# A GRU of 256 steps on one core, without the warm-up matmul that TensorE runs in each step

## The chip, the core and the metric

The kernel runs on one NeuronCore of a Trainium2 chip. The core has four engines that compute: TensorE (PE) for matmuls, VectorE (DVE), ScalarE (ACT) and GpSimd (POOL), and a fifth one, SyncE (SP), which issues transfers. Each engine works off its own list of instructions in order and waits for the others through semaphores. TensorE's clock is granted at one of two levels, 2.4 or 1.2 GHz; the profile writes them as 1.00 and 0.50. The metric is the device time of one execution in microseconds (us).

## The reference, cut to what matters

Two transformer-like layers run over x (4 batches, 256 positions, 256 features) and a vector cond (4 x 256): attention with normalised heads, attention with quantised heads, a resampling with a sparse feed-forward net, then a GRU over the 256 positions, causal attention on its outputs, a small block attention with a layer norm, and a routed feed-forward net. The change touches the GRU alone:

```
def cell(h, x):                      # x: (4, 256) of one position, h: (4, 256)
    gi = x @ W_ih + b_ih             # 256 x 768
    gh = h @ W_hh + b_hh             # 256 x 768
    i_r, i_z, i_n = split(gi, 3);  h_r, h_z, h_n = split(gh, 3)
    r = sigmoid(i_r + h_r);  z = sigmoid(i_z + h_z)
    n = tanh(i_n + r * h_n)
    return (1 - z) * n + z * h
```

The first h is cond. Every position needs the h of the one before, so the 256 steps can't overlap.

## The kernel before

The program has six phases; a barrier between two of them (`next_round`) makes each engine wait for the other three. The GRU is the fourth and has no loop on the chip: its 256 steps are written out, in eight tiles of 32 positions. Its four engines each have a function: `gru_pe`, `gru_act`, `gru_dve`, `gru_pool`.

The four batch rows are too few to fill TensorE's 128 columns. So a gate's 256 outputs are cut into pieces that go to four column groups of 32. `gate` (L827) issues, for each of the two halves of h and each of four column groups, one f32 matmul with 4 columns of weights (the state) and 64 moving columns (a part of W_hh). The trace shows each of these as two records, so the three gates of a step are 48 records, all on L831.

One step t runs like this:

- PE waits for the state (`g_h`) and issues the r gate into one bank, the n gate into the second, the z gate into the third. Each adds to what ScalarE has put there before: the input's share (for n, the bias).
- VectorE transposes the r gate's sums (L969), then the n gate's (L973). ScalarE takes the sigmoid of r (L898).
- VectorE runs a scan that forms i_n + r * h_n in `pre_n` (L978). ScalarE takes the tanh (L906) into `nzh`.
- Meanwhile ScalarE takes the sigmoid of the z gate (L902), and VectorE transposes it (L980).
- ScalarE puts the next step's input shares into the banks (L871, three copies); the first of them stands between L902 and L906 in its order.
- VectorE's last scan (L987) writes the new state into `h_ring` and raises `g_h`; a small product (L942) prepares the next step's `nzh`.

After the z gate PE does one more thing in each step. In seven of the eight tiles, at positions 2 and 4 it does half of the next tile's input matmuls for r and z (`rows_in`, L814, four f32 matmuls with 512 moving columns, eight records), and at positions 6 and 8 those for n (`cols_in`, L821, two f32 matmuls with 128 moving columns, four records). In every other step it runs a warm-up matmul: `keep_warm(1, pM[2])` (L860) issues one bf16 matmul of zeros, 128 x 128 by 512 columns, into a bank that nobody reads in this phase. Its record carries the helper's line, L286. The other phases call `keep_warm` too, with 3, 6 or 8 matmuls at their own places.

Nothing waits for the warm-up matmul, and it waits for nothing; PE works it off in its order, between the z gate of one step and the wait for the next state.

Of the kernel before, what the change touches and what calls it, by code (L numbers as in the profile page):

```python
# [64 lines left out]
def build(nc, d, out):  # L65

    ctx = ExitStack()
    with ctx:
# [84 lines left out]
        pS, pT, pO, pM = bank[0:2], bank[2:4], bank[4], bank[5:8]  # L153
# [119 lines left out]
        def next_round(eng, n):  # L273

            for s in (rd_pe, rd_act, rd_dve, rd_pool):
                eng.wait_ge(s, n)

        def end_round(eng, last, n, rd):

            eng.wait_ge(last, n)  # L280
            eng.sem_inc(rd, 1)

        def keep_warm(n, bank):

            for _ in range(n):
                nc.tensor.matmul(bank[:, :], zero16[:, 0:P], zero16[:, :], start=True, stop=True, skip_group_check=True)  # L286
# [363 lines left out]
        def phase3_pe(pe):  # L650
# [11 lines left out]
            with pe.Fori(0, B) as i:  # L662
# [36 lines left out]
                down(1)  # L699
                end_round(pe, s_down, i * 2 + 2, rd_pe)  # L700
            gru_pe(pe)

        def phase3_act(act):
# [94 lines left out]
        def h_col(t, c):  # L798

            return h_ring[:, h_at(t):h_at(t) + 24].rearrange("p (b x) -> p b x", b=B)[:, :, 3 * c + 2]  # L800
# [9 lines left out]
        def gru_pe(pe):  # L810
            def rows_in(tile, k):
                for b in range(B):
                    at = b * S + tile * TILE
                    mm = nc.tensor.matmul(bank_g[32 * b:32 * b + 32, :], xT[:, k, at:at + TILE], w_ih[:, k, 0:2 * D],  # L814
                                          start=(k == 0), stop=(k == KC - 1), skip_group_check=True)
                if k == KC - 1:
                    mm.then_inc(g_gi, 1)

            def cols_in(tile, m):
                for k in range(KC):  # L820
                    mm = nc.tensor.matmul(bank_i[:, m * P:(m + 1) * P], w_ih[:, k, 2 * D + m * P:2 * D + (m + 1) * P],  # L821
                                          xT[:, k, :].rearrange("p (b s) -> p b s", b=B)[:, :, tile * TILE:(tile + 1) * TILE],
                                          start=(k == 0), stop=(k == KC - 1), skip_group_check=True)
                if m == KC - 1:
                    mm.then_inc(g_ni, 1)

            def gate(t, bank, g, seed, done):  # L827
                pe.wait_ge(seed, t + 1)
                for c in range(KC):
                    for j in range(4):  # L830
                        mm = nc.tensor.matmul(bank[32 * j:32 * j + B, 0:64], h_col(t, c),  # L831
                                              w_hh[:, c, g, :].rearrange("p (m n) -> p m n", m=KC)[:, :, 32 * j:32 * j + 32],
                                              start=False, stop=(c == KC - 1), skip_group_check=True)
                mm.then_inc(done, 1)

            next_round(pe, 13)
            for bank in (bank_r, bank_n, bank_z):
                mm = nc.tensor.matmul(bank[:, 0:64], zero16[:, 0:P], zero16[:, 0:64], start=True, stop=True, skip_group_check=True)
            mm.then_inc(g_open, 1)
            pe.wait_ge(ld_hh, 16)  # L840
            for k in range(KC):
                rows_in(0, k)
            for m in range(KC):
                cols_in(0, m)
            for t in range(S):
                tile, u = divmod(t, TILE)
                pe.wait_ge(g_h, t + 1)
                gate(t, bank_r, 0, g_sdr, g_rm)
                gate(t, bank_n, 2, g_sdn, g_nm)
                gate(t, bank_z, 1, g_sdz, g_zm)  # L850
                if tile + 1 < TILES and u in (2, 4):
                    if u == 2 and tile:
                        pe.wait_ge(g_gd, 4 * tile + 4)
                    rows_in(tile + 1, u // 2 - 1)
                elif tile + 1 < TILES and u in (6, 8):
                    if u == 6:
                        pe.wait_ge(g_nd, tile + 1)
                    cols_in(tile + 1, u // 2 - 3)
                else:
                    keep_warm(1, pM[2])  # L860
            end_round(pe, g_zm, S, rd_pe)
            phase5_pe(pe)

# [131 lines left out]
        def phase5_pe(pe):  # L995
            def project(n, t):

                if t == 0:
                    pe.wait_ge(s_stage3, n)
                for o, w0, w1 in ((pM[t][:, :], 0, 2 * D), (pM[2][:, t * D:(t + 1) * D], 2 * D, 3 * D)):  # L1000
                    for k in range(KC):
                        mm = nc.tensor.matmul(o, aT[:, k, t * P:(t + 1) * P], w_qkv3[:, k, w0:w1],  # L1002
                                              start=(k == 0), stop=(k == KC - 1), skip_group_check=True)
                mm.then_inc(s_qkv3, 1)

            next_round(pe, 14)
            pe.wait_ge(ld_w3, 16)
            for t in range(ST):
                project(1, t)
            with pe.Fori(0, B) as i:  # L1010
                keep_warm(6, pT[0])
                pe.wait_ge(rd_act, i + 14)
                pe.wait_ge(rd_dve, i + 14)
                head_rows(pe, i + 8, extra=6)
                pe.wait_ge(s_vcp, i + 5)
                attn_pe(pe, 8, i, causal=True, ahead=lambda t: project(i + 2, t))
                out_proj(pe, i, 8, w_out3)
                end_round(pe, s_proj, i + 9, rd_pe)
            phase6_pe(pe)
# [564 lines left out]
```

## Time and profile before

| | |
|---|---|
| median of 3 runs | 1282.61 us (1279.76 to 1285.07) |
| the profiled execution | 1276.65 us |
| its span, from the first to the last instruction | 1274.8 us |
| mean granted clock of TensorE | 0.949 |
| PE busy with matmuls | 941.4 us (74%) |
| DVE, ACT, POOL busy | 849.8 us (67%), 521.5 us (41%), 50.9 us (4%) |
| L831, the gates: busy, PE's idle time before them | 221.4 us, 182.7 us |
| L286, all warm-up matmuls: records, busy | 528, 166.8 us |

A line such as "L831 PE MATMUL banks<-w_qkv,h_ring 128*4 128x64 f32 x12288 | 221.4, 221 | 182.7 <-DVE h_ring L987 157.7" is read so: the line of the code, the engine, the operation, what it writes and reads by the program's names (the recurrent weights live in the buffer of `w_qkv2`, hence the name), the shapes, the number of records; then busy time in us and the mean of one in ns; then the idle time of the engine just before them and who ended most of it. The line PEclk shows the granted clock in 40 equal slices of the span, in tenths. In the chain that ended last the profile goes back from the last instruction to what released it, and so on, and gives each line its share of the span.

### The profile page before, as it was taken

The numbers are of one execution on the slowest core, as the hardware profiler recorded it, in microseconds if no ns is written. First come the engines' busy times: TensorE is split into PE (matmuls) and PEld (weight loads), VectorE is DVE, ScalarE is ACT, GpSimd is POOL, SyncE is SP. The second block draws the span as 40 slices with busy tenths as digits, with TensorE's granted clock in tenths as the row PEclk, the third lists the DMA queues.
The fourth block names the chain that finished last, engine by engine and source line by source line (L and its number), as shares of the span: only waits on it lengthen the run. The fifth ranks groups of instructions, "written<-read, shape, count | busy, mean of one in ns | idle before, by whom it ended". The sixth has DMA issues, their size and how long they took to land.

```text
span 1274.8 us, 41104 instructions
## 1 busy us (share of the span) xinstructions
PE 941.4 (74%) x16529; PEld 619.4 (49%) x16529; DVE 849.8 (67%) x2611; ACT 521.5 (41%) x2096; POOL 50.9 (4%) x115
## 2 busy tenths in 40 slices
PE   2899899867877888736666666666666669999836
PEld 2567566434443555514444444444444447776525
DVE  5767576576774666747677776767676657767664
ACT  2435354324441111125555555555555534544211
POOL 0000000022220000100000000000000000000000
PEclk9899999969998999969999999999999999999958
DMA  7000000010001000000000000000000000000101
GB/s 256 3 1 0 0 0 0 0 67 0 0 0 67 0 0 0 33 9 13 4 12 4 13 4 12 4 12 7 10 9 7 4 3 1 0 0 0 34 0 33
DMA packets 32230, 19.77 MB, mean 16 GB/s; under 512 B 23120, under 2 KB 29264, under 8 KB 32080
## 3 DMA queue, kind: packets, MB, share of 16 engines
q1 hardware_dynamic: 32080, 17.64, 4.9%
q8 instruction: 110, 1.80, 0.6%
q14 instruction: 40, 0.33, 0.1%
HBM read 14.49 MB, written 1.05 MB: 12 GB/s over the span
## 4 chain that ended last, share of the span: by engine, by line
PE 38%; DVE 29%; issue 21%; ACT 6%; POOL 2%; DMA 1%; SPq 1%; DVEq 1%; POOLq 0%; ACTq 0%
PE banks L831 9%; PE banks L313 6%; DVE work L973 5%; DVE gate_r L969 5%; DVE h_ring L987 4%; ACT nzh L906 4%; DVE pre_n L978 4%; PE banks L348 3%; PE banks L674 2%; PE banks L1002 2%; PE banks L360 2%; PE banks L1381 2%; PE banks L687 1%; PE banks L286 1%; DVE work L772 1%
## 5 line engine op out<-in xcount | busy, mean ns | idle before, releaser
L831 PE MATMUL banks<-w_qkv,h_ring 128*4 128x64 f32 x12288 | 221.4, 221 | 182.7 <-DVE h_ring L987 157.7
L831 PEld LDWEIGHTS banks<-w_qkv,h_ring 128*4 128x4 f32 x12288 | 173.9, 88 | 266.0 <-DVE h_ring L987 242.8
L286 PE MATMUL banks<-zero 128*128 128x512 bf16 x528 | 166.8, 391 | 10.2 <-DVEq L1554 4.2
L313 PE MATMUL banks<-shared,qT 128*128 128x256 f32 (+2 forms) x640 | 154.3, 349 | 9.4 <-DVE nraw L441 3.6
L898 ACT ACTIVATE zr<-gate_r 128x8 f32<-128x8 f32 x256 | 55.7, 217 | 205.2 <-DVE gate_r L969 205.2
L417 ACT ACTIVATE probs_b<-banks,nraw 128x256 f32<-128x256 f32 (+1 forms) x256 | 100.0, 445 | 76.1 <-DVE nraw L441 43.3
L969 DVE STREAM_TRANSPOSE gate_r<-banks 128x64 f32<-128x64 f32 x256 | 63.9, 250 | 90.8 <-PE banks L831 87.5
L313 PEld LDWEIGHTS banks<-shared,qT 128*128 128x128 f32 (+1 forms) x640 | 95.3, 174 | 30.6 <-DVE nraw L441 12.7
L441 DVE TENSOR_REDUCE nraw<-banks 128x2 f32<-128x512 f32 x128 | 84.9, 686 | 12.0 <-PE banks L313 11.4
L286 PEld LDWEIGHTS banks<-zero 128*128 128x128 bf16 x528 | 50.6, 98 | 68.4 <-issue 21.2
L451 DVE COPY work<-banks 128x512 f32<-128x512 f32 (+1 forms) x104 | 64.1, 616 | 19.9 <-PE banks L360 16.9
L973 DVE STREAM_TRANSPOSE work<-banks 128x64 f32<-128x64 f32 x256 | 76.3, 298 | 0.7 <-PE banks L831 0.7
L348 PE MATMUL banks<-cst,probs_b 128*128 128x128 f32 x448 | 72.2, 278 | 5.0 <-ACT probs_b L417 2.9
L987 DVE TENSOR_TENSOR_SCAN h_ring<-zz,nzh 128x24 f32<-128x24 f32 x256 | 53.2, 208 | 26.6 <-ACT nzh L906 0.5
L980 DVE STREAM_TRANSPOSE zz<-gate_z 128x64 f32<-128x64 f32 x256 | 69.1, 270 | 1.1 <-issue 0.6
L978 DVE TENSOR_TENSOR_SCAN pre_n<-zr,work 128x16 f32<-128x16 f32 x256 | 49.0, 191 | 27.0 <-DVE work L973 0.9
L348 PEld LDWEIGHTS banks<-cst,probs_b 128*128 128x128 f32 x448 | 50.2, 141 | 26.1 <-issue 10.9
L906 ACT ACTIVATE nzh<-pre_n 128x8 f32<-128x8 f32 x256 | 54.8, 214 | 16.7 <-DVE pre_n L978 1.0
L871 ACT COPY banks<-big 128x64 f32<-128x64 f32 x256 | 53.8, 210 | 12.5 <-DMA big<-big 12.5
L902 ACT ACTIVATE gate_z<-banks 128x64 f32<-128x64 f32 x256 | 57.4, 224 | 1.7 <-PE banks L831 1.4
L871 ACT COPY banks<-bhn 128x64 f32<-128x64 f32 x256 | 54.0, 211 | 0.0
L871 ACT COPY banks<-work 128x64 f32<-128x64 f32 x256 | 53.8, 210 | 0.0
(282 smaller groups left out, 1421.2 us busy)
## 6 DMA issues: line engine op xcount, KB each, us to landing
big<-in_x SPq DMA_DIRECT2D x1, 1024.0 KB, 5.6
w_gate<-in_L_ffn_w_gate SPq DMA_DIRECT2D x1, 1024.0 KB, 10.2
shared<-in_L_ffn_w_up SPq DMA_DIRECT2D x1, 1024.0 KB, 5.4
shared<-in_L_ffn_w_down SPq DMA_DIRECT2D x1, 1024.0 KB, 7.9
w_gate<-in_L_ffn_W SPq DMA_DIRECT2D x1, 1024.0 KB, 6.2
big<-big SPq DMA_DIRECT2D x64, 16.0 KB
work<-big SPq DMA_DIRECT2D x64, 16.0 KB
shared<-in_L_ffn_W SPq DMA_DIRECT2D x1, 1024.0 KB, 7.0
```

What stands on the lines that cost most here:

```text
L286: nc.tensor.matmul(bank[:, :], zero16[:, 0:P], zero16[:, :], start=True, stop=True, skip_group_check=True)
L313: mm = nc.tensor.matmul(out, qT[:, c, tile], k[:, c, 0:n], start=True, stop=not causal, skip_group_check=True)
L348: mm = nc.tensor.transpose(pSK[h % 2][:, o:o + P], by_q[h % 3][:, qt * S + kt * P:qt * S + (kt + 1) * P], ident)
L417: a = nc.scalar.activation(by_q[h % 3][:, o:o + n], pSQ[h % 3][:, o:o + n], ACT.Exp, bias=nraw[:, t, h:h + 1])
L441: m = nc.vector.tensor_reduce(nraw[:, :, h], pSQ[h % 3].rearrange("p (t k) -> p t k", t=ST), AX.X, ALU.max, negate=True)
L831: mm = nc.tensor.matmul(bank[32 * j:32 * j + B, 0:64], h_col(t, c), w_hh[:, c, g, :].rearrange("p (m n) -> p m n", m=KC)[:, :, 32 * j:32 * ...
L871: return nc.scalar.copy(bank[:, 0:64], rows).then_inc(done, 1)
L906: nc.scalar.activation(every(nzh[:, :], 0, 3), every(pre_n[:, :], 1), ACT.Tanh, scale=-1.0).then_inc(g_th, 1)
L969: nc.vector.transpose(gate_r[:, :], bank_r[:, 0:64]).then_inc(g_tr, 1)
L973: nc.vector.transpose(blocks(npair[:, 16 * (t % RING):16 * (t % RING) + 128], 0), bank_n[:, 0:64].rearrange("p (m n) -> p m n", m=KC)).the ...
L978: nc.vector.tensor_tensor_scan(pre_n[:, :], zr[:, :], npair[:, 16 * (t % RING):16 * (t % RING) + 16], 0.0, ALU.mult, ALU.add).then_inc(g_p ...
L987: nc.vector.tensor_tensor_scan(h_ring[:, h_at(t + 1):h_at(t + 1) + 24], zz[:, 0:24], nzh[:, :], 0.0, ALU.mult, ALU.subtract).then_inc(g_h, 1)
```

## The change

The `else` branch in the loop of `gru_pe` goes, and with it the call of `keep_warm(1, pM[2])`. In steps without input matmuls PE has nothing between the z gate and the next wait. The other engines' code, the input matmuls and the `keep_warm` calls of the other phases stay.

```diff
--- before.py
+++ after.py
@@ -856,8 +856,6 @@
                     if u == 6:
                         pe.wait_ge(g_nd, tile + 1)
                     cols_in(tile + 1, u // 2 - 3)
-                else:
-                    keep_warm(1, pM[2])
             end_round(pe, g_zm, S, rd_pe)
             phase5_pe(pe)
```

## Rows read from the trace of the kernel before

**Rows 1.** The page: span, granted clock in 40 slices, chain that ended last.
```profile
span 1274.8 us, 41104 instructions
...
PEclk9899999969998999969999999999999999999958
...
PE banks L831 9%; PE banks L313 6%; DVE work L973 5%; DVE gate_r L969 5%; DVE h_ring L987 4%; ACT nzh L906 4%; DVE pre_n L978 4%; PE banks L348 3%; PE banks L674 2%; PE banks L1002 2%; PE banks L360 2%; PE banks L1381 2%; PE banks L687 1%; PE banks L286 1%; DVE work L772 1%
```

**Rows 2.** Groups of instructions, 560 to 1040 us: busy us, mean ns, idle before.
```profile
L831 PE MATMUL banks<-w_qkv,h_ring 128*4 128x64 f32 x12288 | 221.4, 221 | 182.7 <-DVE h_ring L987 157.7 <-ACT banks L871 23.0
...
L286 PE MATMUL banks<-zero 128*128 128x512 bf16 x228 | 89.3, 392 | 0.0
```

**Rows 3.** Line L831 alone: duration min/median/max, first and last start.
```profile
L831 PE MATMUL banks<-w_qkv,h_ring x12288: 219/219/314, 562.0 to 1037.5; 128*4 128x64 f32 x199
```

**Rows 4.** Order of time, one step at the high clock: start us, duration us.
```profile
648.61 0.86 PE L831 MATMUL banks<-w_qkv,h_ring 128*4 128x64 f32 x48 [0.67 <-DVE h_ring L987]
...
649.31 0.30 DVE L973 STREAM_TRANSPOSE work<-banks 128x64 f32<-128x64 f32 x1
...
649.39 0.39 PE L286 MATMUL banks<-zero 128*128 128x512 bf16 x1
...
649.71 0.19 DVE L978 TENSOR_TENSOR_SCAN pre_n<-zr,work 128x16 f32<-128x16 f32 x1
...
650.19 0.21 DVE L987 TENSOR_TENSOR_SCAN h_ring<-zz,nzh 128x24 f32<-128x24 f32 x1
...
650.45 0.86 PE L831 MATMUL banks<-w_qkv,h_ring 128*4 128x64 f32 x48 [0.66 <-DVE h_ring L987]
```

**Rows 5.** Order of time, the loop's second step, at the low clock.
```profile
564.46 1.47 PE L831 MATMUL banks<-w_qkv,h_ring 128*4 128x64 f32 x48 [0.42 <-DVE h_ring L987]
...
565.57 0.30 DVE L973 STREAM_TRANSPOSE work<-banks 128x64 f32<-128x64 f32 x1 [0.18 <-PE banks L831]
...
565.86 0.44 PE L286 MATMUL banks<-zero 128*128 128x512 bf16 x1
565.97 0.19 DVE L978 TENSOR_TENSOR_SCAN pre_n<-zr,work 128x16 f32<-128x16 f32 x1
565.99 0.23 ACT L902 ACTIVATE gate_z<-banks 128x64 f32<-128x64 f32 x1 [0.35 <-PE banks L831]
566.12 0.22 ACT L871 COPY banks<-big 128x64 f32<-128x64 f32 x1
...
566.26 0.21 ACT L906 ACTIVATE nzh<-pre_n 128x8 f32<-128x8 f32 x1
...
566.65 0.21 DVE L987 TENSOR_TENSOR_SCAN h_ring<-zz,nzh 128x24 f32<-128x24 f32 x1
...
566.91 0.85 PE L831 MATMUL banks<-w_qkv,h_ring 128*4 128x64 f32 x48 [0.61 <-DVE h_ring L987]
```

**Rows 6.** Order of time on PE, input matmuls of two steps.
```profile
567.58 1.04 PE L814 MATMUL banks<-w_ih,xT 128*32 128x512 f32 x8
...
578.78 0.71 PE L821 MATMUL banks<-xT,w_ih 128*128 128x128 f32 x4
```

**Rows 7.** Order of time on PE, a step that began later than its neighbours.
```profile
789.31 0.86 PE L831 MATMUL banks<-w_qkv,h_ring 128*4 128x64 f32 x48 [0.97 <-DVE h_ring L987]
```

**Rows 8.** Stretches: busy us (records) of PE, PEld, DVE, ACT, POOL; clock; DMA.
```profile
788.00:791.00 3.00, 1.52 (x53) 0.81 (x50) 2.03 (x10) 1.76 (x12) 0.00 (x0) 1.00 0.04 8
791.50:794.50 3.00, 2.58 (x81) 1.86 (x75) 1.66 (x7) 0.96 (x7) 0.00 (x0) 0.50 0.00 0
337.00:340.00 3.00, 1.63 (x13) 1.01 (x14) 2.73 (x6) 0.10 (x1) 1.21 (x6) 1.00 0.00 0
341.00:344.00 3.00, 2.98 (x16) 1.75 (x15) 2.17 (x5) 1.84 (x4) 0.44 (x3) 0.50 0.00 0
276.00:282.00 6.00, 5.64 (x27) 3.12 (x28) 4.68 (x10) 2.75 (x4) 1.17 (x6) 0.50 0.00 0
562.00:565.50 3.50, 3.04 (x91) 2.35 (x95) 1.66 (x7) 1.20 (x9) 0.00 (x0) 0.50 0.00 0
```

## The prediction

> **What bounds the kernel now.** I read the page first [rows 1]. The span is 1274.8 us, the line of granted clocks stands at 9 from one end to the other apart from single slices, and the chain that ended last goes through L831, the gates' matmuls, at 9%, then through the VectorE and ScalarE lines of the same loop, none of them above 5%. So the GRU is a chain over several engines; no engine is full in it. The groups of instructions between 560 and 1040 us [rows 2] give the counts: 12288 matmul records on L831 are 48 for each of the 256 steps, and 228 warm-up matmuls stand there, one for each step but 28. PE sits idle 182.7 us before L831, and before L286 it never idles. L831 runs from 562.0 to 1037.5 us [rows 3]: 475.5 us for 255 step distances, 1.865 us each, 37% of the span.
>
> Then I read the order of time for one step at the high clock [rows 4] and for one at the low clock [rows 5], because the first two steps of the loop happen to have run at the low one. In rows 4 the reader is to see the ring: L831 starts at 648.61, L973 can read the n gate at 649.31 (0.70 later), L978 runs at 649.71, L987 writes the new state at 650.19, and L831 starts again at 650.45. That is 1.84 us. The warm-up matmul starts at 649.39 and takes 0.39, so it is over at 649.78, and PE then waits 0.66 us for the state. It is on no path: it is PE's last work of the step and the next thing in PE's queue is a wait for L987.
>
> **The change part by part.** It takes 228 matmuls of 0.392 us, 89.3 us of PE's busy time, out of 228 steps [rows 2].
>
> Direct cost of what goes: nothing of it was on the path, so nothing comes back. The cover is 0.66 us of idle time behind each one at the high clock; at the low clock [rows 5] the one at 565.86 is over at 566.30 and PE still waits 0.61 us. Bounds: below, a gain. A few steps of the loop are longer than 1.84 us (L831 at 789.31 came after 0.97 us of idle time, not 0.66 [rows 7]). If every such excess were the warm-up's doing, it would be all of 255 x (1.865 - 1.84) = 6 us, of which some 2 belong to four steps at the low clock; so a gain of 4 us at most. I see no wait of theirs on PE and take 0.
>
> Indirect cost: what PE's clock does. Without the warm-up, PE works 0.86 us in each 1.84, 47%, where it now works 0.86 + 0.39, 68%. What did the engine do before the clock fell elsewhere? In the same loop, from 788 to 791 us, a single longer step brought PE to 1.52 us of 3.00, 51%, with the warm-up still in it, and at 791 the clock went to 0.50 [rows 8]. In another stage PE was busy 1.63 of 3.00 us, 54%, from 337 to 340 us, and from 341 on the clock was at 0.50 [rows 8]. So 47%, step after step, is under two levels at which it fell. I take it that it falls, and soon, in every row of plain steps.
>
> Does it come back? Between 276 and 282 us the clock was at 0.50 with PE busy 5.64 of 6.00 us, 94% [rows 8]; the loop's start shows 3.04 of 3.50 us, 87%, at 0.50, and 791.5 to 794.5 shows 2.58 of 3.00, 86%; the clock rose right behind both. A step at the low clock without the warm-up has 1.47 us of PE in 2.45 (from 564.46 to 566.91 [rows 5]), 60%. That is less than any stretch here after which it rose, so plain steps keep the low clock. The 28 steps with input matmuls are another thing: L814 has eight matmuls, 1.04 us, and L821 four, 0.71 us, at the high clock [rows 6]. At the low one L814 is some 2.1 us, and with the gates' 1.47 PE is full for a whole step. They sit at positions 2, 4, 6 and 8 of each tile of 32, for seven tiles. I expect the clock to rise at the first or second of them, and to stay up a step or two after the last: from position 3 to 10 or 11, 8 or 9 of 32 steps.
>
> A step at the low clock costs 2.45 us (564.46 to 566.91) against 1.84: +0.61. The rows say where. L973 starts 1.11 us behind L831 instead of 0.70, +0.41, since the r and n gates take longer. And L987 starts 0.68 behind L978 instead of 0.48, +0.20, because L902 waits for the z gate to 565.99, then L871 has ScalarE, and L906 starts only at 566.26. Around 791 to 796 the distances were a little shorter, since the clock changed inside them, so I use 0.60.
>
> Sum: 256 steps less 7 x 8.5 = 60 at the high clock leaves 196; four of those are at the low clock already; 192 x 0.60 = 115 us. In one heavy step of each tile L814 runs at the low clock: from about 1.3 us behind the start, 2.1 us long, 3.4 instead of 2.45, +1.0; the clock changes inside some, so seven of these give some 4 us. Together +119. The profiled execution of before took 1276.65 us, 1.85 around its span; plus 119 is 1396. The median of its runs, 1282.61, lies 6 above it. I forecast a median of 1400 us.
>
> A rule of the Trainium skill speaks against this. "TensorE: Matmul & The Clock Gate", section "Why this matters for your kernels", says that throughput drops in the middle of a kernel are avoided by leaving no idle gap of about 3 us between bursts of matmuls. The longest gap in a step here would be about 1 us, so by that rule the warm-up is needless and the time stays at 1283. The trace does not agree: before the fall at 791 us no gap of PE was longer than 0.97 us. I give the rule the chance of the rival below.
>
> **The rivals.**
> The clock stays high. For it: from 562 to 1038 us it did so but for the loop's start and one fall, although PE was idle about a third of the time, and the loop has steps with much more work in each tile. Against it: the fall at 51%. Its place is PE, its price is the 0 to -4 us of above, and it decides if 0.86 us of work in 1.84 are enough. Time 1279 to 1283.
> The clock swings all the time: it falls in plain steps and comes back in plain steps too. For it: at the low clock PE's share rises from 47% to 60% by itself, and that is more than the 54% of the other fall. Against it: the low clock of 276 to 282 us with PE at 94%. If every second step is slow, 126 x 0.60 = 76 us: 1359.
> The clock never comes back after its first fall. Then 252 x 0.61 = 154, plus 14 steps with L814 at +1.0 and 14 with L821 at +0.3 (1.3 + 1.4 = 2.7 against 2.45), 18 us: +172, 1455. Against it: heavy steps fill PE for a whole step, and after full stretches it rose each time.
>
> **How the numbers follow.** Forecast 0.72, swinging 0.12, never back 0.08, stays high 0.08 (0.06 of it no change, 0.02 a gain over 0.5%, for which 6 us would be needed). I take 0.5% as what a measurement of this kernel tells from no change, since its three runs lie within 0.4%. In the forecast itself one step more or less per tile at the high clock is 4 us and a slow step of 0.55 or 0.65 is 10 us; 6 or 12 fast steps per tile make it 1411 or 1385. The range takes in the swinging case: 1345 to 1430. Faster 0.02, same 0.06, slower 0.92.
>
> **What would show it.** In the changed kernel the slices of the GRU should show a clock of 5 to 7 tenths in each, not 9, and a bit higher at each tile's beginning. The groups should have 300 L286 records instead of 528, the mean of L831 well above 221 ns, and the stretch of L831 should be near 595 us, not 475.5. In the order of time plain steps should be 2.4 to 2.45 us apart with L973 1.1 us behind L831. All stages but the GRU should keep their lengths. I am wrong if the GRU's slices stay at 9, and wrong on the size if plain steps without an input matmul run at the high clock far behind position 11 of a tile, or if not even positions 3 to 10 do.

## The result, and the profile after

The kernel without the warm-up matmul took 1394.17 us in the median of six runs (1388.04 to 1401.27), the kernel before beside it 1283.23 us (1279.76 to 1288.15). The ratio is 1.0868, with a 95% interval of 1.0834 to 1.0902: 111 us more. The forecast was 1400 us, with a range of 1345 to 1430. All ratios in this document leave out executions more than 1.5% above the fastest one of the same kernel.

The page of the changed kernel, the same three things as [rows 1]:

```profile
span 1386.2 us, 40620 instructions
...
PEclk9899999799989997757667656556575558999957
...
PE banks L831 22%; PE banks L313 6%; DVE h_ring L985 4%; DVE zz L978 4%; PE banks L348 3%; ACT gate_z L900 3%; PE banks L674 2%; PE banks L1000 2%; PE banks L360 2%; PE banks L1379 2%; DVE work L971 1%; DVE gate_r L967 1%; ACT nzh L904 1%; PE banks L687 1%; DVE pre_n L976 1%
```

The granted clock is 5 to 7 in every slice of the GRU, where it was 9; outside the GRU it is as it was but for single slices (the slice at the GRU's start was low before, too). In the chain, L831 has gone from 9% to 22%. (Lines behind the change stand two numbers lower: L987 is L985 now.)

The line L831 alone, and its group of instructions from the page (busy us, mean ns, idle before), which answer to [rows 3] and [rows 2]:

```profile
L831 PE MATMUL banks<-w_qkv,h_ring x12288: 219/311/314, 562.8 to 1147.2; 128*4 128x64 f32 x199
```
```profile
L831 PE MATMUL banks<-w_qkv,h_ring 128*4 128x64 f32 x12288 | 330.0, 283 | 255.0 <-DVE h_ring L985 229.0
```

From its first to its last record L831 took 1147.2 - 562.8 = 584.4 us, where it took 475.5: 108.9 of the 111.4 us by which the span grew. The median of one record is 311 ns, not 219. The matmuls are the same 12288; they ran mostly at 1.2 GHz (the mean granted clock from 562 to 1149 us is 0.62). Of the 2.5 us left, 0.9 us stands in the first matmuls of the next phase (the 16 of L1000 took 7.85 us, 6.95 before).

How many steps were slow can be read from the waits. At the high clock ScalarE does not wait for the z gate, at the low clock it does; columns are total us, times, longest. Before:

```profile
ACT gate_z L902 <- PE banks L831: 1.4, 4, 0.4
```

After:

```profile
ACT gate_z L900 <- PE banks L831: 64.5, 185, 0.4
DVE work L971 <- PE banks L831: 31.8, 180, 0.2
```

So 180 to 185 steps met the low clock, fully or in part, where 4 did before.

The order of time in one slow step, which answers to [rows 5]:

```profile
700.92 1.47 PE L831 MATMUL banks<-w_qkv,h_ring 128*4 128x64 f32 x48 [0.98 <-DVE h_ring L985]
...
702.02 0.30 DVE L971 STREAM_TRANSPOSE work<-banks 128x64 f32<-128x64 f32 x1 [0.18 <-PE banks L831]
...
702.42 0.19 DVE L976 TENSOR_TENSOR_SCAN pre_n<-zr,work 128x16 f32<-128x16 f32 x1
702.45 0.22 ACT L900 ACTIVATE gate_z<-banks 128x64 f32<-128x64 f32 x1 [0.35 <-PE banks L831]
702.57 0.22 ACT L869 COPY banks<-work 128x64 f32<-128x64 f32 x1
702.70 0.29 DVE L978 STREAM_TRANSPOSE zz<-gate_z 128x64 f32<-128x64 f32 x1
702.71 0.21 ACT L904 ACTIVATE nzh<-pre_n 128x8 f32<-128x8 f32 x1
...
703.10 0.21 DVE L985 TENSOR_TENSOR_SCAN h_ring<-zz,nzh 128x24 f32<-128x24 f32 x1
...
703.36 1.47 PE L831 MATMUL banks<-w_qkv,h_ring 128*4 128x64 f32 x48 [0.98 <-DVE h_ring L985]
```

It is 2.44 us long against 1.84. PE waits 0.98 us of it for the state; its own work, 1.47 us, is the longer part of the ring. The chain that ended last, in the same step:

```profile
700.92 1.51 PE banks L831 x48
702.43 0.02 issue
702.45 0.23 ACT gate_z L900
702.68 0.02 issue
702.70 0.30 DVE zz L978
...
703.10 0.22 DVE h_ring L985
```

Here all 48 records stand in it. In a fast step only the r gate's 16 do, as the chain of the kernel before has it:

```profile
650.45 0.45 PE banks L831 x16
```

The stretches around one tile (the second) show when the clock rose and fell. A heavy step is one with input matmuls, a plain step one without. The first stretch holds the end of the tile before and the tile's start; columns are as in [rows 8]:

```profile
636.00:641.00 5.00, 3.47 (x100) 2.62 (x104) 2.94 (x13) 2.00 (x14) 0.00 (x0) 0.50 0.02 5
645.00:656.00 11.00, 7.21 (x313) 5.14 (x304) 8.02 (x39) 5.79 (x36) 0.00 (x0) 1.00 0.01 3
656.00:664.00 8.00, 3.70 (x219) 2.85 (x204) 5.79 (x28) 4.29 (x26) 0.00 (x0) 1.00 0.02 5
664.00:667.00 3.00, 1.03 (x63) 0.77 (x60) 2.20 (x11) 2.33 (x13) 0.00 (x0) 1.00 0.15 22
670.00:708.00 38.00, 22.47 (x740) 17.89 (x730) 22.00 (x94) 14.98 (x96) 0.93 (x2) 0.50 0.04 6
```

The clock comes up at the input matmuls. PE is then 66% busy until they are done (7.21 of 11.00 us), and in the plain steps behind them 46% and less (3.70 of 8.00 us, then 1.03 of 3.00). The clock stays high for some of these steps and then falls. At the low clock PE is 59% busy (22.47 of 38.00) and stays there for the rest of the tile.

### The profile page after: what moved, and what is told of

Same layout as the page of the kernel before. It is cut to its first block, busy times and chain, and to the rows that moved or that the text cites. A ratio compares the mean times of both kernels' runs of the same rounds, so it can differ in the third digit from the quotient of the medians.

```text
span 1386.2 us, 40620 instructions
## 1 busy us (share of the span) xinstructions
PE 978.4 (71%) x16273; PEld 690.6 (50%) x16301; DVE 873.4 (63%) x2611; ACT 516.6 (37%) x2096; POOL 50.8 (4%) x115
## 4 chain that ended last, share of the span: by engine, by line
PE 49%; DVE 21%; issue 19%; ACT 6%; POOL 2%; DMA 1%; SPq 1%; DVEq 0%; POOLq 0%; ACTq 0%
PE banks L831 22%; PE banks L313 6%; DVE h_ring L985 4%; DVE zz L978 4%; PE banks L348 3%; ACT gate_z L900 3%; PE banks L674 2%; PE banks L1000 2%; PE banks L360 2%; PE banks L1379 2%; DVE work L971 1%; DVE gate_r L967 1%; ACT nzh L904 1%; PE banks L687 1%; DVE pre_n L976 1%
## 5 line engine op out<-in xcount | busy, mean ns | idle before, releaser
L831 PE MATMUL banks<-w_qkv,h_ring 128*4 128x64 f32 x12288 | 330.0, 283 | 255.0 <-DVE h_ring L985 229.0
L831 PEld LDWEIGHTS banks<-w_qkv,h_ring 128*4 128x4 f32 x12288 | 264.7, 112 | 333.3 <-DVE h_ring L985 306.0
L978 DVE STREAM_TRANSPOSE zz<-gate_z 128x64 f32<-128x64 f32 x256 | 73.2, 286 | 16.9 <-ACT gate_z L900 0.6
L900 ACT ACTIVATE gate_z<-banks 128x64 f32<-128x64 f32 x256 | 57.1, 223 | 64.7 <-PE banks L831 64.5
L286 PE MATMUL banks<-zero 128*128 128x512 bf16 x272 | 71.1, 390 | 13.2 <-PE banks L533 4.5
L985 DVE TENSOR_TENSOR_SCAN h_ring<-zz,nzh 128x24 f32<-128x24 f32 x256 | 53.1, 208 | 26.5 <-ACT nzh L904 0.5
L869 ACT COPY banks<-big 128x64 f32<-128x64 f32 x256 | 54.6, 213 | 14.4 <-DMA big<-big 14.4
L869 ACT COPY banks<-bhn 128x64 f32<-128x64 f32 x256 | 55.5, 217 | 0.0
L869 ACT COPY banks<-work 128x64 f32<-128x64 f32 x256 | 54.7, 214 | 0.0
L940 DVE TENSOR_TENSOR nzh<-h_ring,signs 128x16 f32<-128x16 f32 x256 | 44.8, 175 | 10.2 <-ACT zr L884 1.0
```

Source lines behind the costliest of these rows:

```text
L869: return nc.scalar.copy(bank[:, 0:64], rows).then_inc(done, 1)
L900: nc.scalar.activation(gate_z[:, :], bank_z[:, 0:64], ACT.Sigmoid, scale=-1.0).then_inc(g_sz, 1)
L978: nc.vector.transpose(blocks(zz[:, :], 2, 3), gate_z[:, :].rearrange("p (m n) -> p m n", m=KC)).then_inc(g_tz, 1)
L985: nc.vector.tensor_tensor_scan(h_ring[:, h_at(t + 1):h_at(t + 1) + 24], zz[:, 0:24], nzh[:, :], 0.0, ALU.mult, ALU.subtract).then_inc(g_h, 1)
```

## The experiments

Theory W says that the clock follows how much PE streams (how many columns its matmuls move through the array), and that the level of the clock is the whole of the loss. Against it stood: P, that any PE instruction in the idle gap would do; S, that the longest gap decides; G, that each step without a warm-up pays for itself; D, that the loss is not the clock's at all. All ratios are to the kernel before, run beside each.

**A warm-up of 32 columns (e1_cols32).**

```diff
-                    keep_warm(1, pM[2])
+                    nc.tensor.matmul(pM[2][:, 0:32], zero16[:, 0:P], zero16[:, 0:32], start=True, stop=True, skip_group_check=True)
```

> The warm-up matmul stands at its old place in all 228 steps, but with 32 moving columns instead of 512; its weights are loaded as before. Theory W (the clock follows how much of the time PE streams): the idle gap before the next state is broken at the same place, but PE works hardly more than in the changed kernel, so the GRU runs mostly at the low clock and the time is that of the changed kernel, 1385 to 1400 us, with some 180 steps of 2.44 us. Rival P (any PE instruction at that place, or the weight load with it, keeps the clock): about 1283 us, the GRU's slices at 9 tenths. Rival D (what was lost is not the clock but something the instruction did for its neighbours): the steps return to 1.84 us, whatever the clock shows.

Measured: 1393.63 us, ratio 1.0888 (1.0832 to 1.0944). The groups of instructions of this kernel from 560 to 1150 us:

```profile
L831 PE MATMUL banks<-w_qkv,h_ring 128*4 128x64 f32 x12288 | 327.2, 281 | 222.1 <-DVE h_ring L987 198.1 <-ACT banks L871 23.2
...
L860 PE MATMUL banks<-zero 128*128 128x32 bf16 x228 | 46.3, 203 | 0.0
```

All 228 warm-ups are there, each counted as 203 ns busy, and they bring nothing. That rules out P: neither an instruction in the gap nor its weight load keeps the clock. D falls as well: the instruction is back at its place, and yet the records of L831 are at the low clock (281 ns in the mean) and the time stays lost. It also warns of the busy column, which gives the 32 columns 203 ns and the 512 columns 392 [rows 2], though they stream sixteen times as many.

**256 columns (e2_cols256)**, the same edit with 256.

> The warm-up with 256 moving columns instead of 512 in all 228 steps. At the high clock that is some 0.11 us of streaming less of the 0.21 that the full one streams. Theory W in a strict form (the change of clock is a switch and not a slope): half the work does not bring half of the gain. PE's work per plain step is then nearer to that of the changed kernel than to that of the kernel before, the one fall of the kernel before came with a step only 0.3 us too long, and I expect it to fall in nearly every tile and to come back at the input matmuls only: 1375 to 1395 us. Theory W as a slope: half of the 111 us, about 1338 us. Rival P: 1283 us.

Measured: 1289.08 us, ratio 1.0063 (1.0035 to 1.0091). My range of 1375 to 1395 us missed it by 86 us. The strict form had the switch on the wrong side of 256 columns; the slope was wrong too. Half of the warm-up does 93% of its work (8 us lost of 111). The kernel is less even, though: its ten executions lie between 1279.9 and 1309.0 us, and the longest has the lowest mean granted clock, 0.907 against 0.945. The wait of L902 for the z gate came 21 times in this kernel's GRU:

```profile
ACT gate_z L902 <- PE banks L831: 7.2, 21, 0.4
```

**128 and 192 columns (e7_cols128, e9_cols192)**, the same edit, to find the edge.

> The warm-up with 128 moving columns in all 228 steps, between the 256 that kept the clock for nearly all of the loop and the 32 that did nothing. Theory W as a switch: PE then streams 0.05 us more per plain step than in the changed kernel. I expect the clock to fall in each tile as there, perhaps a few steps later, and to come back at the input matmuls or, in some tiles, before: 1350 to 1392 us, nearer to the upper end. If the loss were a slope in the columns, 256 columns at +8 us and 32 at +113 would put 128 at about +68 us, 1348 us.

Measured: 1378.26 us, ratio 1.0747 (1.0701 to 1.0793); 163 such waits. As forecast for a switch (1350 to 1392), and well above the slope (1348).

> The warm-up with 192 moving columns, between the 128 that cost 97 us and the 256 that cost 8. If the loss goes in a switch, one of the two neighbours is repeated or the loop swings between them tile by tile; I expect falls in nearly every tile, but returns inside a tile too, since with 128 columns a few of those were there already: 1300 to 1350 us. On a straight line between the neighbours it would be 1334 us, so this run places the switch and does not prove its form.

Measured: 1365.53 us, ratio 1.0665 (1.0581 to 1.0748), from two executions, and a miss: it is 16 us above my range of 1300 to 1350. It shows the form all the same: by the ratios 0, 32, 128, 192, 256 and 512 columns cost 111, 114, 96, 85, 8 and 0 us. Between 192 and 256 columns there are 77 us, between 0 and 192 there are 26. The waits of L902 with 192 columns:

```profile
ACT gate_z L902 <- PE banks L831: 55.2, 161, 0.4
```

**The full warm-up in every second step (e5_alt).**

```diff
-                else:
+                elif t % 2:
                     keep_warm(1, pM[2])
```

> The full warm-up of 512 columns, but only in every second step (odd ones), so that the loop streams as many warm-up columns as with 256 in every step. Theory W (the clock follows how much PE streams, summed over a few steps): about as the run with 256 columns in each step, a fall now and then and back within some steps, 1283 to 1300 us, with 10 to 30 steps of 2.4 us. Rival G (each step without a warm-up costs by itself): half the steps are slow, 114 x 0.6 = 68 us, 1350 us. Rival S (the longest idle gap decides): the gap is that of the changed kernel in every second step, so the clock falls as there: near 1390 us.

Measured: 1288.81 us, ratio 1.0053 (1.0024 to 1.0081), the same as with 256 columns in every step. G and S fall: every second step has the gap of the changed kernel and costs nothing by itself. It also shows that the share of busy time isn't what decides. In three plain steps ahead of its fall at 598 us, e7_cols128 had PE busy for 3.05 of 5.53 us (from 588.53), 55%; here six plain steps had it busy for 6.11 of 11.06 us (from 836.24), 55% too. The kernel with 128 columns in each step lost the clock in every tile, and this one, which streams twice as many filler columns, kept it nearly throughout. One of its falls, over the end of a tile, in stretches:

```profile
747.00:804.00 57.00, 35.07 (x1498) 24.03 (x1502) 39.80 (x186) 29.82 (x183) 0.93 (x2) 0.96 0.05 8
804.00:813.00 9.00, 6.53 (x186) 4.51 (x178) 5.26 (x22) 3.57 (x24) 0.93 (x2) 0.50 0.01 4
813.00:818.00 5.00, 4.19 (x105) 2.71 (x105) 2.85 (x14) 2.00 (x14) 0.00 (x0) 0.50 0.01 3
818.00:870.00 52.00, 31.64 (x1378) 21.87 (x1374) 35.97 (x169) 27.00 (x165) 0.00 (x0) 0.98 0.05 9
```

At the low clock PE was busy 73% of 9 us, more than the 59% of the changed kernel, and did not come back at once; it came back at the heavy steps behind. Three other falls of this execution, in plain steps, lasted only about 3.4 us each (from 649.2, 679.9 and 908.6 us).

**Left out in the last tile only (e6_last).**

```diff
-                else:
+                elif tile + 1 < TILES:
                     keep_warm(1, pM[2])
```

> The warm-up is left out in the eighth tile only, in the last 32 steps, which have no input matmuls. Theory W: the clock falls within the first few of them (in the changed kernel it fell 11 to 18 steps into a tile, up to seven steps behind the last input matmuls) and has nothing that brings it back: 25 to 31 steps at 2.44 instead of 1.84 us, 15 to 19 us more, 1295 to 1301 us; tiles 1 to 7 as in the kernel before. Rival (the low clock of the changed kernel comes from how the GRU begins, at the low clock, and not from what PE does in a tile): no fall, 1281 us.

Measured: 1295.98 us, ratio 1.0124 (1.0075 to 1.0173), 15 to 16 us. The eighth tile began at 981.0 us:

```profile
560.00:980.00 420.00, 277.97 (x11116) 179.93 (x11116) 292.78 (x1368) 221.81 (x1356) 5.58 (x12) 0.99 0.05 8
980.00:990.00 10.00, 4.84 (x241) 3.53 (x240) 6.99 (x33) 5.44 (x36) 0.94 (x2) 0.94 0.01 3
990.00:1055.00 65.00, 39.10 (x1288) 31.66 (x1292) 37.47 (x160) 24.76 (x159) 0.00 (x0) 0.50 0.01 3
```

The clock was up for some 420 us and fell in the fifth step without a warm-up. The loss is local, and nothing at the loop's start is needed for it.

**Left out beside the input matmuls (e4_near).**

```diff
-                else:
+                elif tile + 1 == TILES or u not in (3, 5, 7, 9):
                     keep_warm(1, pM[2])
```

> The warm-up is left out only at positions 3, 5, 7 and 9 of the seven tiles that have input matmuls at 2, 4, 6 and 8 (28 of 228 steps). Theory W: the input matmuls beside them give PE enough to do, so the clock stays high and the time is that of the kernel before within 0.5%, 1279 to 1288 us; if position 9 is one too many, a fall costs some 2.5 us in a tile and the time is up to 1300 us. Rival (each step without a warm-up costs its own 0.6 us, wherever it stands): 28 x 0.6 = 17 us in 28 steps, 1300 us, with those steps at 2.44 us.

Measured: 1282.71 us, ratio 1.0028 (1.0005 to 1.0050). No change by the bound of 0.5%, though the interval leaves room for 1 to 6 us. G would have had 1.013. Where real work stands near, 28 of the 228 warm-ups together bring 6 us at most.

**Two warm-ups (e3_two)**, `keep_warm(2, pM[2])`, the one version that might beat both kernels.

> Two warm-up matmuls in each of the 228 steps. The second adds some 0.21 us of PE time; PE has 0.66 us of idle time in a step, so the path is not touched. Theory W: no fall inside the GRU any more, behind its first steps; a fall costs 2 to 3 us at the low clock (two steps at +0.54), so the gain over the kernel before is 1 to 8 us, depending on how often that one falls in an execution: 1276 to 1282 us. Rival (the warm-ups lie on the path after all): slower, by up to 0.2 us x 228 = 45 us, 1328 us.

Measured: 1279.62 us, ratio 0.9999 (0.9978 to 1.0021). Another 512 columns are hidden as well, which shows that the warm-ups do not lie on the path, and they gain nothing that can be measured. In its profiled execution the GRU had no fall behind its first two steps, which ran at the low clock; the kernel before loses only a few us to such falls.

**What a slow step is made of (e8_seed_late).** In the changed kernel, the r bank's seed moves behind the tanh:

```diff
-                if t + 1 < S:
-                    seed_r(t + 1)
                 act.wait_ge(g_pn, t + 1)
                 nc.scalar.activation(every(nzh[:, :], 0, 3), every(pre_n[:, :], 1), ACT.Tanh, scale=-1.0).then_inc(g_th, 1)
                 if t + 1 < S:
+                    seed_r(t + 1)
                     seed_nz(t + 1)
```

> The changed kernel (no warm-up) with one more edit on ScalarE: the copy that seeds the r gate's bank (the first of the three L869) is issued behind the tanh (L904) instead of ahead of it. It tells what makes a step at the low clock 0.2 us longer behind the scan L976. The prediction put it on ScalarE: the z gate's sigmoid L900 comes late, then the copy, and the tanh behind both. If that is so, the tanh starts earlier, the state is written earlier and a slow step goes from 2.44 to 2.34 or less: 178 x 0.1 = 18 us less, near 1376 us. Rival Z: the chain of the changed kernel goes from all 48 matmul records through L900 and the transpose of z (L978) to L985, and the tanh is ready earlier; then slow steps stay at 2.44 us and the time at 1390 to 1398 us, although the tanh starts earlier.

Measured: 1393.07 us, ratio 1.0910 (1.0837 to 1.0983), the changed kernel's time.

```profile
702.57 0.19 DVE L975 TENSOR_TENSOR_SCAN pre_n<-zr,work 128x16 f32<-128x16 f32 x1
702.60 0.22 ACT L900 ACTIVATE gate_z<-banks 128x64 f32<-128x64 f32 x1 [0.35 <-PE banks L831]
702.80 0.21 ACT L902 ACTIVATE nzh<-pre_n 128x8 f32<-128x8 f32 x1
702.86 0.29 DVE L977 STREAM_TRANSPOSE zz<-gate_z 128x64 f32<-128x64 f32 x1
...
703.25 0.21 DVE L984 TENSOR_TENSOR_SCAN h_ring<-zz,nzh 128x24 f32<-128x24 f32 x1
```

The tanh starts 0.23 us behind the scan, not 0.29, but the new state is written 0.68 behind it as before. The transpose of z ends last, not ScalarE's tanh.

## Why the prediction was right

- **The warm-up is on no path.** Right. Without it a plain step at the high clock is 1.84 us long, as it was with it, and a second one costs nothing (e3_two). The few longer steps are not its doing either: position 10 of the second tile is 2.20 us long before and 2.19 us after. So the gain of up to 4 us that I allowed for was not there.
- **The clock falls in plain steps.** Right: each of the first seven tiles lost it, and the eighth, without input matmuls, was low throughout. No gap of PE ahead of the fall at 667 us was over 1.34 us, and in the whole loop PE never waited longer than 1.3 us for the state. The order of time on PE ahead of the fall, and the wait (total us, times, longest):

```profile
657.69 0.86 PE L831 MATMUL banks<-w_qkv,h_ring 128*4 128x64 f32 x48 [1.34 <-DVE h_ring L985]
659.54 0.86 PE L831 MATMUL banks<-w_qkv,h_ring 128*4 128x64 f32 x48 [0.99 <-DVE h_ring L985]
...
666.91 1.17 PE L831 MATMUL banks<-w_qkv,h_ring 128*4 128x64 f32 x48 [0.99 <-DVE h_ring L985]
```
```profile
PE banks L831 <- DVE h_ring L985: 229.0, 241, 1.3
```

  The Trainium skill, "TensorE: Matmul & The Clock Gate", section "Why this matters for your kernels", says that drops of throughput in the middle of a kernel are avoided by leaving PE no idle gap of more than about 3 us between bursts of matmuls. This trace does not agree: with gaps of at most 1.34 us the clock fell in each of those seven tiles. And e5_alt has the gaps of the changed kernel in every second step and keeps the clock nearly throughout.
- **47% busy, because the clock fell elsewhere at 51% and 54%.** Right in its outcome, with some luck in the measure. In e5_alt the clock stayed high at 55% busy, in e7_cols128 it fell at 55%, so a busy share alone does not tell whether it falls. That 47% is less than 51% and 54% was no safe argument; that the clock fell is what the trace of the changed kernel shows.
- **It does not come back in plain steps, but at the input matmuls.** Right for six of the seven tiles that have input matmuls, and for the eighth, which has none and stayed low. In the seventh tile it rose one step ahead of them, in plain steps. In e8_seed_late, which leaves PE the same work, it did so in several tiles, for a step or two each time. So "keeps the low clock" was too absolute: with PE about 60% busy at the low clock it mostly stayed there, and rose now and then.
- **192 more slow steps.** 180 to 185 met the low clock, less the 4 of before, so about 176 to 181. I had the clock high until position 10 or 11; in the first three tiles it lasted to 15 or later (in the third, ten steps behind the last input matmuls), the others fell at 10 to 12.
- **0.60 us each.** Right: 2.44 against 1.84. But the second part of it was told wrongly. The 0.20 us behind the scan are not the turn of the seeding copy (L871, now L869) on ScalarE ahead of the tanh. The chain goes through all three gates' matmuls, the sigmoid of z (L900) and its transpose (L978), and with the copy moved away in e8_seed_late the step stayed as long.
- **+4 us for L814 at the low clock.** Close: it costs about 0.5 us and not 1.0 where it happens (1.94 us for its eight matmuls at 640 us, which use up the step's wait for the state; that step is 2.94 us long), and in six tiles, so some 3 us.
- **Sum.** 178 x 0.60 + 3 = 110 us, measured 109 in the GRU and 111 in the span; the forecast had 119. The term that was too large is the number of slow steps. Of the other signs, the 300 warm-ups are there by their weight loads; the trace has only 272 of their matmul records.

The rivals: the clock staying high is out. Swinging in plain steps hardly happened without a warm-up, but it does with 192 columns (161 slow steps, spread in short runs over the tiles), so that rival was near. Never coming back is what e6_last shows for a tile without input matmuls.

Left open: what exactly the chip counts, and why the first tiles kept the high clock longer than the later ones. Every filler tried is a bf16 matmul of zeros at the same place in the step. Other data, types and places were not tried, and the edge between 192 and 256 columns is that of this loop.

## What to carry to other kernels

In a chain of small matmuls, PE's own idle time can be worth nothing and its clock a good deal (111 us of 1283 here). Before deleting work that no engine waits for, read what the granted clock does in the same loop when one step is longer than its neighbours. Price a slow step from a step that the trace has at the low clock, count how many there will be, and look for real work that will bring the clock back. The gain of a filler does not grow evenly with its size. Here half of it, or all of it in every second step, saves 103 or 104 of the 111 us, and three eighths save 26.

## What the runs showed of the hardware

I had not expected the steepness: 77 us lie between a filler of 192 and one of 256 bf16 columns per 1.84 us step, with ratios of 1.0665 and 1.0063. And the busy time of a matmul in the profile is no measure of what keeps the clock: 32 columns show 203 ns and keep nothing, 256 columns show 290 ns and keep nearly all. Two kernels whose plain steps had PE equally busy at the high clock, 55% of the time, differed by 89 us (e7_cols128 and e5_alt).
